# Routing of a two-layer mixture-of-experts kernel done group by group, with roots and weights on GpSimd and weights and list rows loaded in pieces

## The reference, cut to what matters

```python
x = x + 0.5 * ffn(layernorm(x))          # first FFN
x = x + attention(layernorm(x))          # 16 heads, out projection, residual, layernorm * gamma + beta
x = x + 0.5 * ffn(layernorm(x))          # second FFN

def ffn(x):                              # T = 4096 tokens, D = 128, E = 64 experts, K = 8, F = 96, C = 64
    probs = softmax(x @ router_w.T)
    topk_w, topk_ids = top_k(probs, 8);  topk_w /= sum(topk_w)
    # each expert takes the first C = 64 tokens that chose it
    xb = rows of x by expert             # [E, C, D]
    y = (silu(xb @ w_gate) * (xb @ w_up)) @ w_down
    routed = sum over a token's experts of y * topk_w
    shared = (silu(x @ ws_gate) * (x @ ws_up)) @ ws_down
    return routed + shared
```

## Time and profile before

| | |
|---|---|
| median of 3 executions | 964.06 us (962.13 to 964.1) |
| profiled execution, its own time | 963.4 us |
| its span in the trace | 961.6 us |
| busy: PE, DVE, ACT, POOL | 702.0, 635.7, 462.6, 384.7 us |
| granted TensorE clock, mean | 0.817 of 2.4 GHz |
| first FFN, attention, second FFN | about 0 to 244, 244 to 743, 743 to 962 us |

### The profile page before, as it was taken

How to read it: one execution, slowest core, us unless ns; L and a number is a source line. 1 busy time by engine, 2 the same in 40 slices (tenths; PEclk the granted TensorE clock), 3 DMA queues, 4 the chain that set the end, 5 groups by cost and what they waited for, 6 DMA issues and landing times.

```text
span 961.6 us, 16608 instructions
## 1 busy us (share of the span) xinstructions
PE 702.0 (73%) x4710; PEld 354.3 (37%) x4771; DVE 635.7 (66%) x1570; ACT 462.6 (48%) x1007; POOL 384.7 (40%) x480
## 2 busy tenths in 40 slices
PE   0256658783169999999999999999960459388870
PEld 0244347572113333333333333333210444377660
DVE  3289824433478888888888888888817699424430
ACT  0223323331015777777777777777765234133330
POOL 1152657865741333223332233321005426658852
PEclk9999856855558999999999999999995559556755
DMA  8941243332443454444444444445110122523324
GB/s 239 250 107 53 80 143 44 53 39 22 101 92 67 81 94 91 96 88 93 80 89 95 88 93 80 89 95 90 33 46 3 56 71 60 165 37 50 53 25 101
DMA packets 219782, 80.18 MB, mean 83 GB/s; under 512 B 149880, under 2 KB 213528, under 8 KB 219672
## 3 DMA queue, kind: packets, MB, share of 16 engines
q1 hardware_dynamic: 197160, 59.70, 28.7%
q0 software_dynamic: 12288, 10.49, 7.4%
q10 hardware_dynamic: 10288, 9.44, 3.9%
HBM read 49.94 MB, written 31.49 MB: 85 GB/s over the span
## 4 chain that ended last, share of the span: by engine, by line
PE 47%; DVE 18%; DMA 9%; ACT 8%; issue 8%; POOL 5%; ACTq 3%; DVEq 0%; POOLq 0%; SPq 0%
PE psum L1294 13%; PE psum L1285 11%; PE psum L1272 10%; DMA sums<-sums_sb,sidx 6%; PE psum L1208 5%; ACT arena L1067 4%; POOL sums L580 3%; ACTq L965 2%; DVE arena L744 2%; DVE arena L742 2%; PE psum L1181 2%; ACT arena L1014 2%; DVE arena L862 2%; DMA arena<-dispatch_rows,arena 1%; DVE arena L706 1%
## 5 line engine op out<-in xcount | busy, mean ns | idle before, releaser
L862 DVE TENSOR_REDUCE arena<-psum 128x2 f32<-128x1024 f32 x256 | 309.1, 1221 | 51.8 <-PE psum L1272 48.3
L1067 ACT ACTIVATE arena<-psum 128x512 f32<-128x512 f32 x512 | 282.1, 600 | 115.1 <-PE psum L1285 105.1
L1272 PE MATMUL psum<-arena 126*128 126x512 bf16 x512 | 199.8, 397 | 8.7 <-DVE arena L862 4.1
L1285 PE MATMUL psum<-arena 128*128 128x512 bf16 x451 | 173.2, 387 | 7.1 <-ACT arena L1067 3.3
L1294 PE MATMUL psum<-arena 128*32 128x512 f32 x1024 | 136.2, 604 | 1.3 <-ACT arena L1058 1.3
L580 POOL DMA_INDIRECT sums<-sums_sb,sidx x64 | 102.0, 1593 | 62.9 <-DVE sums_sb L810 33.7
L628 POOL CAST arena<-arena 128x256 bf16<-128x256 f32 x32 | 12.7, 396 | 267.5 <-issue 263.5
L1285 PEld LDWEIGHTS psum<-arena 128*128 128x128 bf16 x512 | 50.6, 100 | 150.1 <-ACT arena L1067 122.6
L810 DVE COPY sums_sb<-psum 128x256 f32<-128x256 f32 x32 | 13.6, 424 | 115.9 <-DMA sums<-sums_sb,sidx 65.8
L563 POOL DMA_INDIRECT arena<-dispatch_rows,arena x64 | 62.8, 981 | 26.0 <-issue 13.4
L1014 ACT ACTIVATE arena<-psum,arena 64x128 f32<-64x128 f32 x128 | 46.3, 362 | 45.3 <-PE psum L1181 42.9
(11 more groups left out here) (137 smaller groups left out, 1106.0 us busy)
## 6 DMA issues: line engine op xcount, KB each, us to landing
arena<-qk_parts SPq DMA_DIRECT2D x128, 96.0 KB
ctx<-arena SPq DMA_DIRECT2D x32, 256.0 KB, 2.0
qk_parts<-arena SPq DMA_DIRECT2D x32, 192.0 KB, 3.7
dispatch_rows<-xn_sb SPq DMA_DIRECT2D x16, 256.0 KB, 2.3
sums<-x_sb SPq DMA_DIRECT2D x16, 256.0 KB, 2.3
arena<-lists SPq DMA_DIRECT2D x8, 512.0 KB, 5.7
arena<-qk_parts SPq DMA_DIRECT2D x64, 64.0 KB
arena<-ctx SPq DMA_DIRECT2D x64, 64.0 KB, 2.3
```

The lines of the kernel that those rows point to most:

```text
L862: dve.tensor_reduce(mx_r[r % 2][:, 2 * p:2 * p + 2], src, X, ALU.max).then_inc(a_mx, 1)
L1067: act.activation(p_r[tau % NPB], bank[4 + tau % 2][:, :], ACT.Exp, scale=SCALE).then_inc(a_P, 1)
L1272: ins = pe.matmul(bank[tau % 4][:, :], heads(q_st[r], rows, g)[:, qt * P:(qt + 1) * P], heads(k_st[r], rows, g), start=True, stop=True)
L1285: pe.matmul(bank[4 + tau % 2][:, :], keys, heads(q_st[r], rows, g), start=True, stop=True)\
```

## The change

The diff touches five things.

- Statistics and `normalise`: the reciprocal root is taken by POOL, for the four columns of a group, by an addition of epsilon (`tensor_scalar`) and a power of -0.5 (`tensor_tensor` with a tile `power`). DVE's share is `token_stats` for one group. In the first FFN DVE's program is statistics of group g, then `route(g - 2)`. ACT takes no root any more.
- Routing: DVE takes the negated row maximum; ACT makes the exponentials straight from the logits in PSUM, four activations of 64 columns with the maximum as bias; DVE searches the top eight in the exponentials, marks them with 2, and sums the eight values that it found. The two multiplications that make the weights move to POOL (`weights`).
- The order: POOL does `weights(g - 2)` ahead of `normalise(g)`; PE does the transposes of group g ahead of the logits of group g - 1, and ACT the copies of group g ahead of the exponentials of g - 1.
- The expert weights are loaded on SP's queue, in 24 pieces of 8 experts: one behind each store of the routing in the first FFN, 16 behind the last. The attention weights follow behind them.
- `list_row` is loaded in 8 pieces of 256 KB, of which those behind the first wait for PE's transposes of gathered rows.

```diff
 # POOL
                 def normalise(g, r):
                     xn = xn_sb[:, r, :, :]

                     wait(pool, f.xns[r], 16 * ((g - r) // 2) if isinstance(g, int) else 8 * (g - r))
                     wait(pool, f.xtp, g - 1)
+                    wait(pool, f.aggr, GT * g + GT)
+                    rs = rstd[:, bass.ds(g * GT, GT)]
+                    pool.tensor_scalar(rs, mv[:, bass.ds(g * GT, GT), 1], LN_EPS, None, ALU.add).then_inc(f.ve.sem, 1)
+                    wait(pool, f.ve, g + 1)
+                    pool.tensor_tensor(rs, rs, power[:, 0:GT], ALU.pow).then_inc(f.rs.sem, 1)
                     pool.tensor_tensor(xn, x_sb[:, bass.ds(g * GT, GT), :],
...
+                def weights(g, r):
...
+                    wait(pool, f.key, g + 1)
...
+                    pool.tensor_tensor(w, e_r[r].rearrange("p (j e) -> p j e", j=GT), kk, ALU.mult).then_inc(f.es.sem, 1)
+                    wait(pool, f.es, g + 1)
+                    wait(pool, f.rden, g + 1)
+                    pool.tensor_tensor(w, w, den_r[r].unsqueeze(2).to_broadcast([P, GT, E]), ALU.mult).then_inc(f.w.sem, 1)
...
                 normalise(0, 0)
                 normalise(1, 1)
-                with pool.Fori(1, NG // 2) as i:
-                    for r in range(2):
-                        normalise(2 * i + r, r)
+                for g in range(2, NG):
+                    weights(g - 2, g % 2)
+                    normalise(g, g % 2)
+                weights(NG - 2, 0)
+                weights(NG - 1, 1)
 # DVE, route(g, r)
                     wait(dve, f.lg, g + 1)
-                    dve.tensor_reduce(m_r[r], lg, X, ALU.max).then_inc(f.mx.sem, 1)
...
+                    dve.tensor_reduce(m_r[r], lg, X, ALU.max, negate=True).then_inc(f.mx.sem, 1)
                     for j in range(GT):
-                        dve.tensor_scalar(d[:, j, :], lg[:, j, :], m_r[r][:, j:j + 1], -88.0,
-                                          ALU.subtract, ALU.max).then_inc(f.d.sem, 1)
+                        wait_apart(dve, (f.ex, g + 1))
+                        dve.max(top[:, j, :], e[:, j, :]).then_inc(f.top.sem, 1)
...
+                    dve.tensor_reduce(den_r[r], top, X, ALU.add).then_inc(f.den.sem, 1)
                     wait(dve, f.rep, GT * (g + 1))
...
-                    dve.scalar_tensor_tensor(out=e_r[r], in0=d_r[r], scalar=0.5, in1=e_r[r],
-                                             op0=ALU.is_gt, op1=ALU.mult).then_inc(f.es.sem, 1)
...
-                    dve.tensor_reduce(den_r[r], e, X, ALU.add).then_inc(f.den.sem, 1)
...
+                    dve.tensor_scalar(den_r[r], den_r[r], 2.0, None, ALU.mult).then_inc(f.den2.sem, 1)
 # ACT
+                def exps(g, r):
+                    wait(act, f.mx, g + 1)
...
+                    for j in range(GT):
+                        ins = act.activation(e_r[r][:, j * E:(j + 1) * E], bank[2 + r][:, j * E:(j + 1) * E], ACT.Exp,
+                                             bias=m_r[r][:, j:j + 1])
+                    ins.then_inc(f.ex.sem, 1)
 # PE
-                route(0, 0)
-                route(1, 1)
+                transposes(0, 0)
...
+                transposes(1, 1)
+                logits(0, 0)
                 with pe.Fori(1, NG // 2) as i:
                     for r in range(2):
-                        route(2 * i + r, r)
+                        transposes(2 * i + r, r)
+                        logits(2 * i + (r - 1), 1 - r)
+                logits(NG - 1, 1)
 # SP
+                if f.p == 0:
+                    for g in range(NG):
+                        store(g, g % 2)
+                        if g:
+                            store_w(g - 1, (g - 1) % 2)
+                        expert_weights(g)
+                    store_w(NG - 1, 1)
+                    for c in range(NG, 24):
+                        expert_weights(c)
+                    attention_weights()
...
-                for c in range(NQ // 4):
...
+                for c in range(NQ // 2):
+                    part = slice(c * 4 * P, (c + 1) * 4 * P)
+                    wait(sp, f.gtp, 2 * c - 3 if c > 1 else c)
```

More of the change, by code:

```diff
@@ L122, in macaron_kernel @@
         rstd = sb("rstd", [P, NT])
+        power = sb("power", [P, NT])
         xn_sb = sb("xn_sb", [P, 2, GT, D])
@@ L241, in macaron_kernel @@
             totals[f"base_stored{i}"] = 16 * NG // 2
-        for i in range(4):
+        for i in range(NQ // 2):
             totals[f"lists_loaded{i}"] = 16
@@ L286, in __init__ @@
                 self.lst, self.lsd = n("slots_listed"), n("lists_stored")
-                self.lrow = [n(f"lists_loaded{i}") for i in range(4)]
+                self.lrow = [n(f"lists_loaded{i}") for i in range(NQ // 2)]
                 self.base = [n(f"base_stored{i}") for i in range(2)]
@@ L372, in store_w @@
                       .then_inc(f.ws[r].sem, 16)
[L373 to L376, removed]
-                    for r in range(2):
-                        store(2 * i + r, r)
-                        store_w(2 * i + (r - 1), 1 - r)
-                store_w(NG - 1, 1)
+                if f.p == 0:
[8 more added lines that the diff above has]
+                    attention_weights()
+                else:
+                    store(0, 0)
+                    store(1, 1)
+                    store_w(0, 0)
+                    with sp.Fori(1, NG // 2) as i:
+                        for r in range(2):
+                            store(2 * i + r, r)
+                            store_w(2 * i + (r - 1), 1 - r)
+                    store_w(NG - 1, 1)
                 def store_base(g, r):
@@ L725, in ffn @@
-                with dve.Fori(1, NG // 2) as i:
-                    for r in range(2):
-                        route(2 * i + r, r)
+                dve.wait_ge(s_cst, 4)
+                if f.p == 0:
+                    for g in range(NG):
+                        if g % 2 == 0:
+                            dve.wait_ge(s_x[g // 2], 16)
+                        token_stats(f, g)
+                        if g == 1:
+                            dve.wait_ge(s_rwp, 1)
+                            dve.tensor_copy(rwT[:], bank[7][:, 0:E]).then_inc(s_rws, 1)
+                        if g > 1:
+                            route(g - 2, g % 2)
+                    route(NG - 2, 0)
+                    route(NG - 1, 1)
+                else:
+                    route(0, 0)
+                    route(1, 1)
+                    with dve.Fori(1, NG // 2) as i:
+                        for r in range(2):
+                            route(2 * i + r, r)
@@ L961, in _, with transposed @@
         def _(act):
-            for c in range(4):
-                act.wait_ge(s_x[c], 16)
-            for w, t in ((w_gate, wg_sb), (w_up, wu_sb), (w_down, wd_sb)):
-                act.dma_start(t[:], w.rearrange("e k n -> k e n")).then_inc(s_wexp, 16)
             def ffn(f):
-                wait(act, f.ve, 1)
-                act.activation(rstd[:], rstd[:], ACT.Sqrt).then_inc(f.sd.sem, 1)
-                def route(g, r):
+                def transposed(g, r):
                     wait(act, f.xtp, g + 1)
@@ L1029, in attention @@
             def attention():
-                def std(first, last, count):
-                    act.wait_ge(a_ve, count)
-                    act.activation(rstd[:, first:last], rstd[:, first:last], ACT.Sqrt).then_inc(a_sd, 1)
-                std(0, GT, 1)
                 def xT_copy(t, r):
@@ L1104, in ffn, with transposes @@
             def ffn(f):
-                def route(g, r):
+                def transposes(g, r):
                     wait(pe, f.xn, g + 1)
@@ L1110, in route, with logits @@
                     ins.then_inc(f.xtp.sem, 1)
+                def logits(g, r):
                     wait(pe, f.xts, 2 * g + 1)
-                    wait(pe, f.d, GT * (g - 1))
+                    wait(pe, f.ex, g - 1)
                     for j in range(GT):
```

156 lines of the change are left out of this document (70 added, 86 removed).

## The result

The changed kernel takes 1016.92 us (median of 4; 1016.32 to 1017.93) against 963.1 (961.61 to 964.1) for the kernel before beside it: a ratio of 1.0561, 95% interval 1.0541 to 1.0581. It is slower, as forecast, but by 5.6% and not by 3.4%: 996.8 us was too low, and so was the upper end of 1014. The profiled execution took 1016.32 us with a span of 1014.4; that of before has a span of 961.6. So 52.8 us of span have to be found, where 33.4 were forecast.

What follows compares the result with a forecast made beforehand. Routing was taken as bound by a four-engine ring, one group per lap of 11.0 or 11.3 us. Terms +3.9, +34.3, -4.0, +0.5, -1.3 made +33.4 on 963.4: 996.8 us, range 984 to 1014.

Steps and rivals of the forecast that it cites:

- The ring: Routing of both FFNs: closed chain through PE, DVE, ACT and POOL, one group per lap, 11.0 and 11.3 us.
- The terms of the lap: Routing: durations of one lap's steps on PE, DVE, ACT and POOL, summing to 11.0 us (first FFN) and 11.3 (second).
- epsilon and power on 4 columns: POOL's normalise: two small operations in no row, likeliest 0.14 us each, at most 0.5 each.
- rival 3: POOL's normalise: epsilon and power cost 1 us each, 27 us more in all, so 1024 us; chance 0.10.
- the last routes: End of routing: route(6), two small operations and route(7) after six laps, 7.5 us in the first FFN, 8.1 in the second.
- The z root: Attention's end: moving the root to POOL saves 0.2 us at most, left out of the sum.
- the fourth part: From attention's last aggregation to the second FFN's first row maximum: forecast 3.8 us shorter.
- Attention's own start: From the four aggregations to the first centering, and again for 28 tiles ahead of the first row maxima: -1.3 us.
- Weights on SP: First FFN: 16 expert pieces, then attention weights, behind the last routing store on SP's queue: +0.5 us.
- rival 2: The queue: SP held at issue until pieces land at 112.2, base stores done at 131.4; +8 us, 1004; chance 0.10.
- List pieces: Gather stages: only 256 KB of list rows ahead of the second gather, -2.0 us per FFN, -4.0 in all.
- rival 1: Routing: the same closed chain with sizes off, lap 10.0 to 12.2 us, total 984 to 1011; chance 0.75.

Runs made afterwards that it cites:

- e1: Changed kernel with POOL doing normalise(g) ahead of weights(g - 2): 961.15 us, ratio 0.9894 to the kernel before.
- E2: Changed kernel with a product in place of the power in the routings' normalise, root left out: 1013.87 us, ratio 1.0446 to the kernel before.
- e4: Changed kernel with the root at attention's end back on DVE and ACT, as before: 1024.59 us, ratio 1.0552 to the kernel before.
- e3: Changed kernel with three expert pieces behind each routing store and attention weights behind the list rows on SP: 1022.81 us, ratio 1.0531 to the kernel before.
- e6: Kernel before with only the list rows loaded in eight 256 KB pieces with waits: 958.83 us against 963.02, ratio 0.9954.
- c1: The changed kernel again, no edit, on another chip: 1028.24 us, ratio 1.0613 to the kernel before.
- c2: The kernel before again, no edit, for its profile on that other chip: 969.32 us, ratio 1.0005.

## Why the prediction was wrong

- **The ring: right.** The chain through four engines closed as worked out from the order on POOL and PE, with laps of 11.2 us in the first FFN and 11.6 in the second (forecast 11.0 and 11.3), and e1 shows that the order alone makes it: 69 us by the rows, 70 by the ratios.
- **The terms of the lap: one far too small, the others a little too large.** The step that failed is "epsilon and power on 4 columns ... the likeliest 0.14". The nearest row was an iota, which is no arithmetic, and I capped even the bound at 0.5. Epsilon took 0.23 and the power 1.04; rival 3 had 1 for each, and so was right for the power alone. Sixteen `normalise` of 3.45 us and not 2.52 bring +15 us; the lap's other terms gave 8 back (12 laps of 11.18 and 11.63 less the 3.45, against 8.43 and 8.73) and the last routes 1. That the lap of the first FFN came out as forecast is luck in this: the terms missed in both directions. E2 shows the power's price: 14 us by the rows, 16 by the ratios.
- **The z root: "like swap saves 0.2 at most; left out" failed.** It costs 5.1 us by the rows (6 by e4's ratio). The same wrong price stood behind it, now times 32 columns. With two powers in the first two `normalise` (1.9) and 1.0 us by which L537 and L540 ran slower there while DVE was busy, it makes the 7.8 us of the fourth part. Attention's own start did not win its 1.3 either: from the four aggregations to the first centering pass 1.65 us and not 1.23 as before, and 28 columns took 4.83 us.
- **Weights on SP: +0.5 failed, by 6 to 8 us.** I let SP issue base stores without a price for the issues ahead of them, and gave rival 2 one chance in ten. From last key to first gather pass 41.8 us, where 35.9 were forecast (35.4 before) and e3 has 34.6. The 16 pieces held SP at issue for 19.8 us, and the 13 attention DMAs for 9.3 more. Rival 2 had the cause, but not its course: it let SP go on when the pieces have landed, at 112.2; SP went on at 111.75 and they landed near 118. That its 131.4 for the base stores stands beside a first gather at 131.81 is partly luck, since the last key was 2.2 us later than forecast.
- **List pieces: right in size, -4.0 against -4.2 in e6,** but only where nothing else holds the start of the gather stage, and partly by cancellation: PE has the second gather 3.6 us sooner and not 2.0. In the changed kernel's profile the first FFN's loop gave 2.0 of 3.5 us back: it lasts 98.0 us and not 96.0 from first scatter to last.
- **The range** took rival 1 and the queue as alternatives. They were not: power, queue and z root are independent, each can be there with the ring, and all three were. The low end of rival 1 is also a little off: 11.0 less its own two terms is about 10.3 and not 10.0, so 987 us and not 984.

By part of the table the misses are 2.2, 6.4, 1.5, 7.8, 1.9 and -0.4: 19.4 us together. By the rows of the profile after, the three causes are 14.9 (16 powers and epsilons), 5.9 (from last key to first gather) and 5.1 (the z root), 25.9 together; 9 were given back by the lap's other terms and the last routes. The slower L537 and L540 (1.0), attention (1.5), the first FFN's gather stage (2.0 in the loop less 1.5 won at its start) and the last part (-0.4) bring it to 19.5. E2 to e4 confirm the three causes, each to about 3 us; the small terms are read from rows and have no experiment.

## What to carry to other kernels

Follow the order on each engine round until it comes back to itself: two lines in the wrong order cost 70 us here, with no engine more than half busy in that stretch. An operation for which no row exists must be bounded by its kind of arithmetic and its number of columns, and the wrong price goes into every place where the operation stands. Risks that can occur together belong in the range as a sum, and a transfer put on a busy queue costs what stands behind it there.

## What the hardware showed beyond that

- GpSimd's power costs by the column: 1.04 us for 128x4, 4.83 for 128x28, 5.46 for 128x32, so about 0.16 us per column and 0.41 beside it. A product on 128x4 took 0.20. The Trainium skill (GPSIMD Engine Reference, "Engine selection") gives a factor of about 2 against VectorE for elementwise operations of two inputs. The rows of the changed kernel agree with it: 128x512 takes 1.04 us (L545) to 1.26 (L696) on GpSimd and 0.66 on VectorE (L977) where nothing slows them. At 128x4 the power is 5 times a product on the same engine.
- On two chips ScalarE waited 7 to 11 us for something unnamed in each gather stage, in both kernels, until some 13 to 20 us after the first gather; on a third, and in the first two profiles, never there. Its cause stays open. The Trainium skill (Runtime: NRT & Kernel Launch, "Instruction fetch mechanics") says that a sequencer loads its instructions by a DMA queue of its own, so a fetch held up behind gathers would be a candidate. The profiles speak against it: no packet of the instruction queues starts in any of the four waits of c1 and c2; around c1's first wait (140.6 to 151.5 us) there is none from 118 to 163 us.
